# Mask products in the tiling of the scores, and routed weights kept in SBUF with a reordered second attention, in a four-layer transformer kernel

## The reference, cut to what matters

```
x = ln(x + attention0(x))   # 16 heads of 64; rows 0-127 see keys 0-127, rows 128-255 see keys up to their own
x = ln(x + experts0(x))     # 8 experts, the best 2 per token: down(silu(gate x) * (up x))
x = ln(x + attention1(x))   # 16 heads of 8, latent keys and values, rotary; no mask
x = ln(x + experts1(x))     # 8 experts, best 2: w2 gelu(w1 x + b1) + b2, and 2 shared experts
```

```
top = (i < n // 2) & (j < n // 2)
bot = (i >= n // 2) & (j <= i)
scores = where(top | bot, scores, -inf)
```

## Time and profile before

| | |
|---|---|
| median of 3 runs | 1486.32 us (1484.36 to 1487.42) |
| profiled execution, its own time | 1484.3 us |
| its span | 1482.5 us |
| mean granted TensorE clock | 0.966 |
| PE busy | 1318.5 us (89%) |
| DVE busy | 990.1 us (67%) |
| ACT busy | 937.9 us (63%) |
| POOL busy | 620.1 us (42%) |

### The profile page before, as it was taken

The page is one execution under the profiler, slowest core; times in us unless marked ns, Lnnn a source line. Parts: engine busy times, 40 slices in busy tenths (PEclk is TensorE's granted clock), DMA queues, the critical chain, the costliest instruction groups (busy, mean ns, idle before and its releaser), DMA issues. The chain is left out here.

```text
span 1482.5 us, 33826 instructions
## 1 busy us (share of the span) xinstructions
PE 1318.5 (89%) x10654; PEld 1079.4 (73%) x10655; DVE 990.1 (67%) x3104; ACT 937.9 (63%) x2431; POOL 620.1 (42%) x978
## 2 busy tenths in 40 slices
PE   6999999999999999579999569999998998867876
PEld 5777777777777777479999557677776775656765
DVE  5777777777777777546666478888888885432223
ACT  4666666666666666345656347777777776746653
POOL 1234444444433444323433443355555543335653
PEclk9999999999999999889999869999999999989998
DMA  7202021111111110021211340222115000057635
GB/s 240 73 24 72 29 69 32 61 40 54 47 50 52 45 56 8 12 57 54 58 54 48 116 149 12 72 86 76 45 59 191 11 12 16 12 147 198 186 103 178
DMA packets 67400, 107.64 MB, mean 73 GB/s; under 512 B 11521, under 2 KB 52737, under 8 KB 64961
## 3 DMA queue, kind: packets, MB, share of 16 engines
q1 hardware_dynamic: 56800, 86.67, 19.0%
q0 software_dynamic: 9088, 18.89, 3.7%
q10 hardware_dynamic: 1440, 1.19, 0.3%
HBM read 85.74 MB, written 62.06 MB: 100 GB/s over the span
## 5 line engine op out<-in xcount | busy, mean ns | idle before, releaser
L369 POOL TENSOR_TENSOR a_prob<-a_prob,a_rl 128x128 f32<-128x128 f32 (+1 forms) x256 | 128.3, 521 | 299.5 <-DVE a_rl L462 296.7
L262 ACT ACTIVATE a_prob<-psum,a_nmx 128x128 f32<-128x128 f32 (+1 forms) x512 | 209.8, 419 | 14.8 <-DVE a_nmx L457 14.8
L2154 DVE TENSOR_REDUCE a_nmx<-psum 128x2 f32<-128x512 f32 x256 | 169.3, 687 | 30.1 <-PE psum L1451 27.9
L299 ACT ACTIVATE a_probt<-psum 128x768 f32<-128x768 f32 x128 | 103.8, 811 | 79.2 <-PE psum L716 79.2
L859 POOL DMA_INDIRECT yt<-m_yrow,m_dest x78 | 74.9, 960 | 130.9 <-ACT m_yrow L934 119.0
L1819 ACT ACTIVATE a_prob<-psum 128x1024 f32<-128x1024 f32 x128 | 127.5, 1024 | 2.6 <-PE psum L1481 2.4
L1451 PE MATMUL psum<-k_stk,a_q_stk 96*128 96x256 f32 x512 | 118.7, 325 | 11.7 <-DVE a_nmx L2154 5.8
L307 ACT ACTIVATE a_ot<-psum,a_bias 128x256 f32<-128x256 f32 x128 | 61.0, 476 | 100.8 <-PE psum L745 99.7
L456 DVE TENSOR_REDUCE a_nmx<-psum 128x2 f32<-128x256 f32 x128 | 54.3, 424 | 95.7 <-PE psum L652 95.7
L1451 PEld LDWEIGHTS psum<-k_stk,a_q_stk 96*128 96x128 f32 x512 | 80.2, 197 | 49.8 <-issue 24.3
L716 PE MATMUL psum<-ident,a_prob 128*128 128x128 f32 x768 | 105.3, 273 | 10.7 <-DVE a_prob L466 10.7
(11 more groups left out here) (350 smaller groups left out, 3874.5 us busy)
## 6 DMA issues: line engine op xcount, KB each, us to landing
xs<-in_fill SPq DMA_DIRECT2D x144, 264.0 KB, 4.1
m_w<-in_wr SPq DMA_DIRECT2D x39, 321.0 KB
m_xrow<-xs SPq DMA_DIRECT2D x78, 132.0 KB
w<-in_w SPq DMA_DIRECT2D x16, 256.0 KB, 3.5
a_yin<-yt SPq DMA_DIRECT2D x16, 256.0 KB, 2.7
f_yin<-yt SPq DMA_DIRECT2D x7, 512.0 KB, 7.8
yt<-m_yrow,m_dest POOLq DMA_INDIRECT x156
xs<-in_fill_idle SPq DMA_DIRECT2D x2, 1056.0 KB, 7.6
```

The lines of the kernel that those rows point to most:

```text
L262: last = nc.scalar.activation(prob[:, slot, h, at], S[:, 2 * slot + h, at], ACT.Exp, bias=nmx[:, slot, q, h:h + 1], accum_out=lsum[:, slot ...
L299: nc.scalar.activation(probt[:, hp % 2], PT[:, :, 0:SW], ACT.Copy).then_inc(pt_done, 1)
L369: last = nc.gpsimd.tensor_tensor(prob[:, slot, 0, at], prob[:, slot, 0, at], rl[:, slot, 0, q:q + 1].to_broadcast(prob[:, slot, 0, at].sha ...
L2154: nc.vector.reduce_max(nmx[:, :, h:h + 1], bank.rearrange("p (q k) -> p q k", q=QB), AX.X, negate=True).then_inc(mx_done, 1)
```

## The change

Three edits.

**First attention.** The mask is added by four products instead of two, each with 64 rows: the identity and the mask are cut into two bands of 64 rows each (c = 0, 1), held twice, once for each head's half of the rows. `mask32` and `mask` become 128x2x2x128 (identity and mask, band, column); the separate cast of the identity goes, and two waits count one less.

**Second attention.** `tail_heads` gets its banks as an argument (banks 2 and 3 of `ST`, those of the second-pass scores) and moves ahead of `first(1)`; `first(2)` and the router move ahead of `scores(1)`, and a wait for `o_done` stands there; `tail_columns` uses R1; `ranks` moves between heads 14 and 15, `maxima` behind the last outputs. Head 2 uses R0 (`IN_R1`). DVE and ACT follow in the same order. `k_stk` becomes a list of two buffers of the same shape; the first one's memory is later that of `g.w1`.

**Second routed stage.** SP loads the whole `wr1` (8 experts, 128x642 fp32 each) in two DMAs once the last batch's first second-pass scores are counted, into `g.w1`. In routed1 the per-block weight DMA goes. DVE copies the up part of the block's expert (128x256 fp32) into one of four slots `wu`, two blocks ahead; the down part, and the biases, are read in place with an offset from the table, which PE, ACT and DVE each load into a register (DVE twice per block).

```diff
-    mask32 = sb("mask32", [P, P])
-    mask = sb("mask", [P, P], BF16)
-    identb = sb("identb", [P, P], BF16)
+    mask32 = sb("mask32", [P, 2, 2, P])
+    mask = sb("mask", [P, 2, 2, P], BF16)
...
             def masks():
-                dve.wait_ge(ident_in, 16)
-                nc.vector.tensor_copy(identb[:], g.ident[:]).then_inc(consts, 1)
                 dve.wait_ge(mask_in, 16)
                 nc.vector.tensor_copy(mask[:], mask32[:]).then_inc(consts, 1)
...
-                for out, q, k in heads:
-
-                    last = nc.tensor.matmul(out[:, 2 * P:SW], identb[:], mask[:], start=False, stop=True)
+                for c in range(2):
+                    for h in range(2):
+                        at = slice(h * DK0, (h + 1) * DK0)
+                        last = nc.tensor.matmul(heads[h][0][:, 2 * P:SW], mask[at, 0, c, :], mask[at, 1, c, :], start=False, stop=c == 1)
                 last.then_inc(sc_ps, 1)
...
-    XSLOTS, WSLOTS, YSLOTS = 8, 8, 8
+    XSLOTS, WSLOTS, YSLOTS = 8, 4, 8
...
-            def weights(j):
-                after(sp, y_done, j - WSLOTS + 1)
-                sp.dma_start(w[:, j % WSLOTS, :], d["wr1"][:, bass.ds(at(w_at, j, (E1 - 1) * W1R), W1R)]
-                             ).then_inc(w_in[j % WSLOTS], 16)
-
-            weights(0)
-            for j in range(-2, N):
-                if 0 < j:
-                    weights(j)
-                if j + 2 < N:
-                    rows(j + 2)
+            for j in range(N):
+                rows(j)
...
             def up(j):
                 pe.wait_ge(x_done, j + 1)
                 after(pe, act_done, j - 1)
-                pe.wait_ge(w_in[j % WSLOTS], (j // WSLOTS + 1) * 16)
+                pe.wait_ge(w_done, j + 1)
...
             def down(j):
+                w = offset(mybir.EngineType.PE, j)
                 pe.wait_ge(act_done, j + 1)
...
             def units(j):
+                w = offset(mybir.EngineType.Activation, j)
                 act.wait_ge(up_ps, j + 1)
...
+            def weights(j):
+                w = offset(mybir.EngineType.DVE, j)
+                after(dve, up_ps, j - WSLOTS + 1)
+                nc.vector.tensor_copy(wu[:, j % WSLOTS, :], g.w1[:, bass.ds(w, F1)]).then_inc(w_done, 1)
+
             def output(j):
+                w = offset(mybir.EngineType.DVE, j)
                 dve.wait_ge(down_ps, j + 1)
...
+            weights(0)
+            weights(1)
             for j in range(N + 1):
+                if j + 2 < N:
+                    weights(j + 2)
                 if j < N:
                     destinations(j)
...
-    IN_R1 = (0, 1, 2, 3, 5, 6, 8, 11, 13, 15)
+    IN_R1 = (0, 1, 3, 5, 6, 8, 11, 13, 15)
+    OS = (ST[:, 2, :], ST[:, 3, :])
...
+            sp.wait_ge(st_ps, (B - 1) * NPR)
+            for half in range(2):
+                part = slice(half * E1 // 2 * W1R, (half + 1) * E1 // 2 * W1R)
+                sp.dma_start(g.w1[:, part], d["wr1"][:, part]).then_inc(w_in, 16)
+            sp.wait_ge(w_in, 32)
...
                     if turned:
                         turn()
+                    tail_heads(n + 1, OS)
                     first(1)
                     pe.wait_ge(v_done, n + 1)
                     pe.wait_ge(mt_done, n + 1)
                     scores(0, p)
                     if second:
                         pe.wait_ge(stack_act, n * 3 + 6)
-                        pe.wait_ge(mx_done, n * H1 + H1 + 2)
-                    tail_heads(n + 1)
-                    scores(1, p)
-                    pe.wait_ge(exp_done, n * NPR + 1)
-                    scores(2, p)
                     if routed:
                         pe.wait_ge(nt_done, n)
-                    tail_columns(n + 1, R0)
                     first(2)
                     if routed:
                         router(columns_of(n - 2), PV)
+                    pe.wait_ge(o_done, n + 1)
+                    scores(1, p)
+                    if second:
+                        pe.wait_ge(mx_done, n * H1 + H1 + 2)
+                    tail_columns(n + 1, R1)
+                    pe.wait_ge(exp_done, n * NPR + 1)
+                    scores(2, p)
...
-                    first(14, 15)
+                    first(14)
+                    if routed:
+                        pe.wait_ge(osb_done, n * NGR + 4)
+                        ranks(n - 1, PV)
+                    first(15)
...
                     if routed:
-                        pe.wait_ge(osb_done, n * NGR + 4)
-                        ranks(n - 1, PV)
-                    if second:
-                        pe.wait_ge(exp_done, n * NPR + 7)
-                        maxima(n + 2)
-                    if routed:
                         pe.wait_ge(rk_done, n - 1)
                     outputs(NGR - 1, p, n)
+                    if second:
+                        maxima(n + 2)
...
                     maximum(0)
                     if fresh:
                         incoming_variances(n + 4)
-                    maximum(1)
                     if turned:
                         dve.wait_ge(stack_ps, n * NGR + 2 * NGR)
                         rotate_q_rest(n + 3)
-                    tail_heads(n + 1)
+                    tail_heads(n + 1, OS)
+                    maximum(1)
...
+        with nc.sbuf_tensor("k_stk0", [P, H1, T], F32R) as first:
+            pass
+        g.w1 = keep("w1", [P, E1 * W1R])
+        g.k_stk = [first, keep("k_stk1", [P, H1, T], F32R)]
```

More of the change, by code:

```diff
@@ L1025, in routed1 @@
     x_in = [sem(f"x_in{k}") for k in range(XSLOTS)]
-    w_in = [sem(f"w_in{k}") for k in range(WSLOTS)]
+    w_done = sem("w_done")
     y_out = [sem(f"y_out{k}") for k in range(YSLOTS)]
@@ L1033, in after, with offset @@
             eng.wait_ge(signal, n)
+    def offset(engine, j):
+        return nc.values_load(w_at[0:1, j:j + 1], engines=(engine,), min_val=0, max_val=(E1 - 1) * W1R,
+                              skip_runtime_bounds_check_because="the table's rows are clamped")
     with nc.Block(no_gpsimd_drain=True) as block:
@@ L1323, in attention1 @@
                for a, b in ((0, W), (W * GT, 2)))
-    hid_h, hid_l = (flat(k_stk[:, 1])[:, a * W * GT:(a + 1) * W * GT].rearrange("p (d n) -> p d n", n=GT) for a in range(2))
+    hid_h, hid_l = (flat(k_stk[1][:])[:, a * W * GT:(a + 1) * W * GT].rearrange("p (d n) -> p d n", n=GT) for a in range(2))
     TB = NB1 + 1
@@ L1360, in attention1 @@
         "up_ps", "act_done", "hi_done", "hid_done", "down_ps", "ye_done", "er_ps", "added"))
-    count_ps, table = sem("count_ps"), sem("table")
+    count_ps, table, w_in = sem("count_ps"), sem("table"), sem("w_in")
     UP = [ST[:, 0, :], ST[:, 1, :], ST[:, 2, :]]
@@ L1480, in scores @@
                     for k in range(QB):
-                        last = nc.tensor.matmul(out[:, k * T:(k + 1) * T], k_stk[:, p, h, k * P:(k + 1) * P], q_stk[:, p, h // HG, :],
+                        last = nc.tensor.matmul(out[:, k * T:(k + 1) * T], k_stk[p][:, h, k * P:(k + 1) * P], q_stk[:, p, h // HG, :],
                                                 start=True, stop=True)
@@ L1494, in outputs, with tail_heads @@
                 last.then_inc(pv_ps, 1)
-            def tail_heads(n):
+            def tail_heads(n, banks):
                 pe.wait_ge(osb_done, n * NGR - (NGR - 1))
@@ L1500, in tail_heads @@
                     for k in range(NGR):
-                        last = nc.tensor.transpose((R0, R1)[q][:, k * P:(k + 1) * P], osb[:, k, q * P:(q + 1) * P], g.ident[:])
+                        last = nc.tensor.transpose(banks[q][:, k * P:(k + 1) * P], osb[:, k, q * P:(q + 1) * P], g.ident[:])
                 last.then_inc(o_ps, 1)
@@ L1803, in stacks @@
                 for j in range(HG):
-                    nc.scalar.activation(k_stk[0:KR, p, k * HG + j, :], bank[0:KR, T:2 * T], ACT.Identity, scale=in_head[0:KR, j:j + 1])
+                    nc.scalar.activation(k_stk[p][0:KR, k * HG + j, :], bank[0:KR, T:2 * T], ACT.Identity, scale=in_head[0:KR, j:j + 1])
                 nc.scalar.activation(q_stk[0:KR, p, k, :], bank[0:KR, 0:T], ACT.Copy).then_inc(stack_act, 1)
@@ L1812, in markers @@
             def markers(p):
-                nc.scalar.activation(k_stk[KR:P, p], pick[KR:P, :].unsqueeze(2).to_broadcast([P - KR, H1, T]), ACT.Copy)
+                nc.scalar.activation(k_stk[p][KR:P], pick[KR:P, :].unsqueeze(2).to_broadcast([P - KR, H1, T]), ACT.Copy)
             def exps(t, n):
@@ L2160, in split_maxima, with tail_heads @@
                                         ).then_inc(nmx_done, 1)
-            def tail_heads(n):
+            def tail_heads(n, banks):
                 dve.wait_ge(o_ps, n)
-                by_head = [r.rearrange("p (h e) -> p h e", h=H1) for r in (R0, R1)]
+                by_head = [r.rearrange("p (h e) -> p h e", h=H1) for r in banks]
                 for q in range(QB):
@@ L2341, in batches @@
                         route(p, n - 1)
-                    maximum(12, 13, 14, 15)
+                    maximum(12, 13, 14)
```

(9 more changed lines are left out.)

27 lines of the change are left out of this document (13 added, 14 removed).

## The result

The changed kernel takes 1479.58 us (median of 11 runs, 1474.93 to 1482.63) against 1486.32: the medians differ by 6.7 us, and the ratio estimated from all the runs is 0.9946 (95% interval 0.9933 to 0.9959), some 8 us. The forecast was 1461, 25 us faster, with a range of 1446 to 1477. The profiled execution is one of 1479.58 us, with a span of 1477.9 against 1482.5: the two traces differ by 4.6 us.

A forecast was written before the change was run, and what follows sets the result against it. TensorE bounds both attentions (35 us idle in the second), a chain over several engines the second routed stage. Terms +0.3 - 6 - 15 - 4 = -25 against 1484.3 give 1459.3, as a median 1461 us; range 1446 to 1477.

The forecast's parts named there:

- ACT's chain of exps, which fixes the start of a batch and isn't touched: Second attention: the exps set each batch's start and stay unchanged while DVE's chain comes 1.0 us earlier per batch.
- a rival (0.15, -3 and 1473): Second attention: ACT's exps or late PE signals during POOL's scatters take the gain back; -3 for -15, 1473; chance 0.15.
- -15: Second attention: the new order brings DVE's chain 1.0 us earlier per batch, in 15 of 16 batches; bounds -35 to +2.
- the product and cast of L2118 to 1088.5: Second attention, one batch reworked: DVE ends these at 1088.5 instead of 1089.55.
- just in time: Second attention: after POOL's scatters and two operations, the key's low half (L1970) is taken just in time at 1088.5.
- 64 x 0.10: First attention: 64 head pairs each save 0.10 us by one change of tiling less, -6 us; bounds 0 to -10.
- One of the five comes where DVE is the later anyway: First attention: of five pairs in eight followed by L741, one gains nothing, so 64 of 80 are counted.
- -4 was forecast: Second routed stage: 5 to 6 from DMA relief, 2 from row loads, +4 for copies; -4 us (-15 to +12).
- The relief of the DMA engines: Second routed stage: fewer weight DMAs speed up the blocks, worth 0 to 9.5 us, taken as 5 to 6.
- The comparison of 3.25 with 2.90 per block: Second routed stage: L1204 blocks take 3.25 us at DMA share 0.68, 2.90 at 0.22 where weights have ended.
- The slower rival: Second routed stage: DVE's plain fp32 copies hold back POOL's scatters, 0.75 us a block; +29 for -4, 1495; chance 0.07.
- +0.3 for the larger mask load: Kernel start: the four times larger mask load and its longer cast delay only the first scores, +0.3 (0 to +1).

The follow-up runs named there:

- late_exp2: Changed kernel; ACT's first exp of each second-attention batch waits for POOL's power operation behind the four scatters; 1.0049 against the kernel before, on a late-signal chip.
- split_again: Same kernel as split, run on a chip with late signals; 0.9858 against the kernel before, -20 to -21 us.
- split: Changed kernel; POOL's four scatters in the second attention cut in two by the power and the query's low half; 0.9851 against the kernel before, -22 us.
- again: The changed kernel unaltered, on the chip without late signals; 0.9883 against the kernel before, -17 us (1436.58).
- a_only: Kernel before with the mask change alone, on the chip without late signals; 0.9977 against the kernel before, -3.4 us.
- b_only: Kernel before with only the resident weights, copies and split of `k_stk`, on the chip without late signals; 0.9991 against the kernel before.
- pause: Changed kernel; an extra POOL addition behind the scatters of each of the second routed stage's first 29 blocks; 0.996 against before, +11.7 us against again.
- c_again: Same kernel as c_only, run on a chip with late signals; 0.996 against the kernel before.
- before_late: Kernel before; ACT's first exp of a batch waits for POOL's bare increment behind its four scatters; 0.9989 against the kernel before, on a late-signal chip.
- c_only: Kernel before with the reordered second attention alone, on the chip without late signals; 0.9933 against the kernel before, -9.7 us.

## Why the prediction was wrong

The measured 1479.58 lies 2.6 above the range. Of the 25 us, 8 came.

**The chain of exps.** The step that failed is in the second attention: "ACT's chain of exps, which fixes the start of a batch and isn't touched". It is touched. The transposes were put ahead of scores(0) on TensorE, so scores(0) ends 3.1 us after the first scatter and not 1.9. On a chip without late signals this costs 0.7 on the exp (3.2 for 2.5) and is more than paid for behind it. On the chip of the result it puts scores(0)'s signal into the third scatter, where TensorE's signals come late, and the exp starts at 4.25 to 4.9. late_exp2 shows that the exp has no slack, split_again that a shorter run lets it start at 3.2 and brings the whole forecast gain: (381.0 - 363.0)/16 = 1.1 us per batch. I had the mechanism before me, in the routed stage's "remote" waits, had put it as a rival (0.15, -3 and 1473) and took it for the less likely, because the moved work no longer *ran* late; I did not ask into which microsecond of the run each signal would now fall. -3.8 measured for this stage, against -15. Of the 11.2 that are missing, the same kernel on the other chip tells which are the chip's: it gains 11.4 there, so 7.6 are the late signals, and 3.6 are the next point.

**DVE and POOL side by side.** The second failed step is "the product and cast of L2118 to 1088.5": priced with the durations of an order in which POOL did nothing beside them. The new order lays them on POOL's low half, 0.57 us per batch on the chip without late signals (the cast 0.29 to 0.62) and less on the other (the sum 0.47, the cast 0.42). Avoiding the meeting (split against again) brings 4.2 us, 0.26 per batch, so that about half of DVE's loss was hidden. The forecast called POOL "just in time" and did not ask what DVE and POOL would do to each other side by side.

**The mask.** Right in mechanism: one emptying of the array less, 0.54 to 0.43 from L646 to L650, and the same step behind it. Mis-sized: 64 x 0.10; it is 0.22 per batch, -3.3 (-3.4 in a_only), because the shortened scores were the cover of ACT's copy L298 in the first and seventh pair, and of DVE in the sixth. "One of the five comes where DVE is the later anyway" should have been checked on ACT too. In the profiled pair of executions even this was hidden by a half-clock stretch at the start that comes and goes from run to run.

**The routed stage.** -4 was forecast, +3.4 came in the loop, -1.6 at its head and -2.3 behind it: about nothing, and b_only says the same (0.9991) on the other chip. The relief of the DMA engines was worth nothing: where signals are prompt, POOL's issue of 78 scatters is the bound (pause), and where they are late it is also the stall of each third block (POOL idles 2.2 to 2.8 us, twelve times in the changed kernel), which came with 0.28 of DMA share as with 0.61. The comparison of 3.25 with 2.90 per block, on which the 5 to 6 rested, compared stretches that differed in the shared steps too. The slower rival (copies in POOL's way) did not happen on the chip where copies overlap 34 scatters. It took the wrong partner: of the 3.4 us of the loop 2.3 are scatters behind DVE's 128x512 subtraction, an operation that the kernel before has too, at other moments. Whether copies and offset reads moved it there stays open. On one chip with late signals the scatters take 1450.9 - 1324.7 = 126.2 in c_again, without copies, and 128.2 to 130.2 in the three runs with them; on another, 123.9 in before_late and 125.7 and 126.0 in the two with them. So this stretch is some 2 to 4 us longer with the part there, and the same on the chip without late signals (98.1 and 98.2).

**What stays open**: why TensorE's signals are late on some chips and not on others. The runs show only when. No run shows either the forecast's +0.3 for the larger mask load by itself.

The best version is split: 0.9858 and 0.9851 on the two kinds of chip, against 0.9946 and 0.9883 of the changed kernel.

## What to carry to other kernels

When work is moved, lay each *signal* it makes on the other engines' timelines, not only its own start and end: a product moved ahead of another delays the other's signal, and here that signal fell into a run of scatters. Durations are those of an order: check what DVE and POOL will do side by side in the new one. And before pricing an instruction's removal from a bounded engine, look which copy elsewhere it was covering.

## What the runs showed of the hardware that was not expected

- On some chips, while POOL issues scatters nearly back to back (most of all from the third on), an idle ACT or DVE takes TensorE's product 0.3 to 3.7 us behind its end, often only about when the run ends. What waits for DVE's or ACT's signals inside the same runs starts 0.03 to 0.06 us behind their end in most cases. On one chip none was late in any of eight traces, and the same kernel was 32 to 36 us faster there (1454 against 1486 to 1490), 25 of it in the second routed stage.
- The same reordering of the same work gains 0.7% on one chip (c_only) and 0.4% on another (c_again).
- A scatter that starts 0.05 to 0.44 us behind the start of DVE's 128x512 subtraction in SBUF (0.69 us) takes 1.25 to 1.48 us in place of 0.96; a 128x256 copy beside it (0.29 us) leaves it at 0.96.
- DVE's 128x256 addition and cast in SBUF took 668 and 615 ns beside a POOL operation in SBUF, 418 and 294 without, and POOL's 889 for 732.
- A wait for a bare semaphore increment behind POOL's scatters did not hold ACT until they were through (2.4 us before the last one's end in before_late); a wait for a compute operation behind them did (late_exp2).
- After an idle of 2.4 us, TensorE came back at 1.2 GHz in one execution and at 2.4 GHz in another of the same chip (c_again and late_exp2: a granted clock of 0.66 and 1.00 from 20 to 30 us).
